# Where the gated y of a state-space mixer is kept, and who splits off its low part

## What is computed

```
for g in 8 groups, b in 2 sequences of 512 steps:
    proj   = h @ in_proj_w.T                  # gate, channels, B, C of this group
    hid,B,C = silu(causal_conv(proj, 4 taps)) # 1024 channels; B and C have 128
    y      = Y_diag + Y_off + D * hid         # chunked scan, 16 heads of 64 channels
    yg     = y * silu(gate)
    r      = rsqrt(mean(yg*yg over the group) + eps)
    out   += (yg * gnorm_w) @ out_proj_w.T * r
```

## Time and profile before

| | before |
|---|---|
| median of 3 runs | 2004.83 us (2001.99 to 2005.57) |
| the profiled execution: its time, its span | 2006.6 us, 2004.8 us |
| TensorE busy | 1951.4 us (97%) |
| VectorE busy | 1601.0 us (80%) |
| ScalarE busy | 1484.1 us (74%) |
| GpSimd busy | 1230.7 us (61%) |
| granted TensorE clock, mean | 0.996 |
| chain of waits that ended last | PE 76%, DVE 2% |
| y_lo on VectorE (L2140) | 128 instructions, 750 ns each |

### The profile page before, as it was taken

The page is one execution under the profiler, slowest core; times in us unless marked ns, Lnnn a source line. Parts: engine busy times, 40 slices in busy tenths (PEclk is TensorE's granted clock), DMA queues, the critical chain, the costliest instruction groups (busy, mean ns, idle before and its releaser), DMA issues.

```text
span 2004.8 us, 32751 instructions
## 1 busy us (share of the span) xinstructions
PE 1951.4 (97%) x10846; PEld 1567.6 (78%) x10846; DVE 1601.0 (80%) x2979; ACT 1484.1 (74%) x2986; POOL 1230.7 (61%) x854
## 2 busy tenths in 40 slices
PE   7998999999999999999999999999999999999998
PEld 5564666677888888888888888888888888888886
DVE  7777889857777878788878787878787878787888
ACT  5345866547787878787878787878787878787876
POOL 5644777644656666666656666565656665656666
PEclk9998999999999999999999999999999999999999
DMA  5615332544434343334333333333433333433424
GB/s 194 191 55 152 100 92 88 154 149 134 129 97 132 93 132 102 125 113 127 119 115 119 106 119 106 119 118 111 128 114 115 116 109 116 156 108 117 128 92 133
DMA packets 114472, 241.74 MB, mean 121 GB/s; under 512 B 23681, under 2 KB 24706, under 8 KB 113794
## 3 DMA queue, kind: packets, MB, share of 16 engines
q1 hardware_dynamic: 110466, 227.06, 36.2%
q0 software_dynamic: 3840, 12.59, 2.2%
HBM read 226.75 MB, written 12.85 MB: 120 GB/s over the span
## 4 chain that ended last, share of the span: by engine, by line
PE 76%; DVE 2%; ACT 0%; issue 0%; DVEq 0%; ACTq 0%
PE s_ps L75 13%; PE s_ps L77 13%; PE s_ps L76 13%; PE s_ps L1871 6%; PE s_ps_o L75 6%; PE s_ps_o L77 6%; PE s_ps_o L76 6%; PE s_ps L1835 5%; PE s_ps L1879 4%; PE s_ps L1827 3%; PE s_ps L1813 1%; PE s_ps L1861 0%; DVE s_cv L2110 0%; PE s_ps L1819 0%; DVE s_state L2086 0%
## 5 line engine op out<-in xcount | busy, mean ns | idle before, releaser
L2292 POOL TENSOR_TENSOR w_lo<-w_raw,w_hi 128x1024 fp32r<-128x1024 f32 x142 | 340.0, 2399 | 529.7 <-ACT w_hi L1942 529.7
L75 PE MATMUL s_ps<-h_hi,w_hi 128*128 128x512 f32 x1152 | 463.0, 402 | 6.0 <-DVE s_hid L2115 4.2
L77 PE MATMUL s_ps<-h_hi,w_lo 128*128 128x512 f32 x1152 | 450.1, 391 | 0.0
L76 PE MATMUL s_ps<-h_lo,w_hi 128*128 128x512 f32 x1152 | 448.7, 390 | 0.0
L2110 DVE SCALAR_TENSOR_TENSOR s_cv<-s_ps,s_par,s_cv 128x511 f32<-128x511 f32 (+2 forms) x480 | 355.8, 744 | 15.2 <-ACT s_cv L1985 9.3
L2309 POOL TENSOR_TENSOR s_lm<-s_lm,s_cbt 128x512 f32<-128x512 f32 x256 | 326.2, 1296 | 12.2 <-ACT s_lm L1967 12.2
L1960 ACT ACTIVATE s_lm<-s_rows,s_steps 128x128 f32<-128x128 f32 x1024 | 312.5, 391 | 0.8 <-PE s_ps L1871 0.8
L1985 ACT ACTIVATE s_cv<-s_ps,s_par 128x512 f32<-128x512 f32 x160 | 124.5, 778 | 215.8 <-PE s_ps L77 215.8
L75 PEld LDWEIGHTS s_ps<-h_hi,w_hi 128*128 128x128 f32 x1152 | 216.4, 188 | 53.9 <-DVE s_hid L2115 5.6
L77 PEld LDWEIGHTS s_ps<-h_hi,w_lo 128*128 128x128 f32 x1152 | 216.2, 188 | 47.3
L76 PEld LDWEIGHTS s_ps<-h_lo,w_hi 128*128 128x128 f32 x1152 | 216.8, 188 | 41.1
(11 more groups left out here) (295 smaller groups left out, 4106.3 us busy)
## 6 DMA issues: line engine op xcount, KB each, us to landing
w_raw<-in_w_in SPq DMA_DIRECT2D x144, 512.0 KB, 3.7
s_rows<-acs_dram SPq DMA_DIRECT2D x256, 256.0 KB, 4.6
s_wo_raw<-in_w_out SPq DMA_DIRECT2D x128, 256.0 KB, 3.5
w_raw<-in_gu_q SPq DMA_DIRECT2D x14, 512.0 KB, 3.6
f_d_q<-in_d_q SPq DMA_DIRECT2D x28, 256.0 KB, 2.7
f_d_w<-in_d_s SPq DMA_DIRECT2D x28, 256.0 KB, 3.5
table<-shifted SPq DMA_DIRECT2D x16, 256.0 KB, 2.7
xs<-in_x SPq DMA_DIRECT2D x8, 256.0 KB, 6.5
```

The source lines that it names most:

```text
L75: nc.tensor.matmul(dst, l_hi, r_hi, start=start, stop=False)
L76: nc.tensor.matmul(dst, l_hi, r_lo, start=False, stop=False)
L77: return nc.tensor.matmul(dst, l_lo, r_hi, start=False, stop=stop)
L2292: nc.gpsimd.tensor_tensor(w_lo[:, slot, :], w_raw[:, slot, :], w_hi[:, slot, :].bitcast(F32), ALU.subtract).then_inc(w_lo_ready, 1)
```

## The change

`dve_y_gated` now writes its result to SBUF, over the channel tile `hid[:, k, :]` that `dve_y_skip` has read for the last time, where before it wrote back into the DIAG bank. `y_hi` and `sq` read it there. In all units but the last, ScalarE then multiplies that tile in place by `gnorm_w` (`act_scaled`, a new instruction behind `act_sq`), and GpSimd forms `y_lo` as a plain difference (`pool_y_lo`, new); VectorE no longer does. In the last unit `y_lo` stays on VectorE and there is no `act_scaled`. The DIAG bank is free once `y_gated` is done (`y_ready`). `dve_silu` of a channel tile waits until `y_lo` of the tile that it overwrites is done.

```
-        freed = {**took, "DIAG": y_lo_ready, "H": tile_ready, "SQ": ssq_took}
+        freed = {**took, "DIAG": y_ready, "H": tile_ready, "SQ": ssq_took}
...
+        def act_scaled(act, un, k):
+            nc.scalar.activation(gated(un, k), gated(un, k), ACT.Copy,
+                                 scale=par[:, un.b, 58 + k:59 + k]).then_inc(scaled_ready, 1)
...
                     act_sq(act, un, k)
+                    if not un.last:
+                        act_scaled(act, un, k)
...
         def dve_silu(dve, v, i, th):
             dve.wait_ge(th_ready, v.at(NCONV, i))
+            if CONVS[i] >= 2 and not v.first:
+                dve.wait_ge(y_lo_ready, (v.u - 1) * KC + CONVS[i] - 1)
...
         def dve_y_lo(dve, un, k):
-            if un.last and k == KC - 1:
-                dve.wait_ge(y_hi_ready, un.at(KC, k))
-            else:
-                dve.wait_ge(sq_ready, un.at(KC, k))
+            dve.wait_ge(y_hi_ready, un.at(KC, k))
...
         def gated(un, k):
-            return tg[:] if un.last and k == KC - 1 else bank(un, ("DIAG", 0, k))
+            return hid[:, k, :]
...
-                if un.scans:
+                if un.last:
                     dve_y_lo(dve, un, k)
...
         def pool_sum(pool, un, k):
-            pool.wait_ge(sq_ready, un.at(KC, k))
+            pool.wait_ge(scaled_ready, un.at(KC, k))
...
+        def pool_y_lo(pool, un, k):
+            pool.wait_ge(scaled_ready, un.at(KC, k))
+            nc.gpsimd.tensor_tensor(y_lo[:, k % 2, :], gated(un, k), y_hi[:, k % 2, :].bitcast(F32),
+                                    ALU.subtract).then_inc(y_lo_ready, 1)
...
                     pool_wo(pool, un, k)
+                    if not un.last:
+                        pool_y_lo(pool, un, k)
                     if k and not (un.last and k == KC - 1):
                         pool_sum(pool, un, k)
```

More of the change, by code:

```diff
@@ L1589, in mixer @@
         y_lo_ready = sem("s_y_lo_ready")
-        sq_ready = sem("s_sq_ready")
+        scaled_ready = sem("s_scaled_ready")
         ssq_ready = sem("s_ssq_ready")
@@ L1932, in pe_last @@
                 if t == 0:
-                    pe.wait_ge(sq_ready, v.at(KC, KC - 1))
+                    pe.wait_ge(scaled_ready, v.at(KC, KC - 1))
                     pe_squares(sq[:, (KC - 1) % 2, :], sums, False, True).then_inc(ssq_done, 1)
@@ L2013, in act_sq @@
                 act.wait_ge(ssq_ready, un.u * (KC - 1))
-            nc.scalar.activation(sq[:, k % 2, :], gated(un, k), ACT.Square).then_inc(sq_ready, 1)
+            ins = nc.scalar.activation(sq[:, k % 2, :], gated(un, k), ACT.Square)
+            if un.last:
+                ins.then_inc(scaled_ready, 1)
+        def act_scaled(act, un, k):
+            nc.scalar.activation(gated(un, k), gated(un, k), ACT.Copy,
+                                 scale=par[:, un.b, 58 + k:59 + k]).then_inc(scaled_ready, 1)
         def act_wo(act, un, k):
@@ L2191, in gated @@
         def gated(un, k):
-            return tg[:] if un.last and k == KC - 1 else bank(un, ("DIAG", 0, k))
+            return hid[:, k, :]
         def dve_y_gated(dve, un, k):
             dve.wait_ge(y_chain, (un.u * KC + k) * 2 + 2)
-            if un.last and k == KC - 1:
-                dve.wait_ge(took["G"], UNITS * KC)
             nc.vector.tensor_tensor(gated(un, k), bank(un, ("DIAG", 0, k)), gate[:, k, :],
```

## The result

The changed kernel takes 2022.88 us, the median of four runs (2021.81 to 2025.46). The kernel before takes 2004.56 us (2001.99 to 2005.57; four runs on the same chip, three of which were those known ahead of the prediction). The ratio is 1.0095, with a 95% interval of 1.0078 to 1.0113: 18.3 us slower. The forecast was 2023 us.

What follows compares the result with a forecast made beforehand. The prediction took the mixer to be bound by TensorE, with ScalarE's full stretches in slots 0 and 2 passed on to it. Its terms sum to 17.9 us: 2024.5 for the profiled execution, 2023 us for the median, range 2011 to 2031.

Steps and rivals of the forecast that it cites:

- x: Delay per slot on ScalarE from the new activation and two reads from SBUF: 0.70 us, bounds 0.48 and 0.85.
- Slot 2: C's tap, convolutions and `silu` come later and TensorE's last projection waits: 0.71 us in each of 15 units, 10.6 us.
- Slot 1: Slot 0's gate waits for its tanh on ScalarE, delaying `yoff`, ST and T: 0.35 us in 14 units, 4.9 us.
- The -0.4 us for DIAG: DIAG no longer waits for `y_lo` to free its bank: a gain counted as 0.4 us in all.
- GpSimd: Its 120 new differences fit into its waits for `w_hi`: cost nothing, at most 0.5 x 14 = 7 us.
- The last unit: `y_lo` on VectorE, both inputs in SBUF, and GpSimd delay each other; GpSimd's round grows to 6.9: 2.5 us, bounds 0 and 8.
- The sums of unit 14: Four VectorE sums on L1723 in unit 14 meet a busier GpSimd: 0.3 us more.
- The sum: All terms over the kernel: 10.6 + 4.9 - 0.4 + 2.5 + 0.3 = 17.9 us slower.
- hidden: Rival, 7%: ScalarE's wait for TensorE covers the activation in slot 2 too; only the gate's 0.35 or less remains; 2004 to 2008.
- VectorE's release decides: Rival, 6%: the activation costs ScalarE almost nothing, freed VectorE brings slot 1's gate and `yoff` forward: 4.2 us faster, 2000.5.
- GpSimd is late: Rival, 7%: `y_lo` misses slot 1's output product or its port waits reach VectorE in all units: up to 7 us more, 2030.

Runs made afterwards that it cites:

- two-scalings kernel: The changed kernel with a second activation of the same form ahead of the in-place scaling in units 0 to 11, its output unread; ratio 1.0157 to the kernel before.
- three moves: The changed kernel with C's tap (slot 2) and the gate's tanh (slot 0) ahead of `y_hi`, and the last unit's y in PSUM; ratio 0.9978 to the kernel before.
- the early tap: The kernel before, with the tap of C ahead of `y_hi` and the square on ScalarE in slot 2; ratio 1.0067, and 0.9987 with `y_lo` behind C's `silu`.

## Why the prediction was right, step by step

**x, the delay on ScalarE**: 0.70 us predicted. By the groups (against the earlier trace rows):

```profile
L2005 ACT ACTIVATE s_y_hi<-s_hid,s_par 128x512 fp32r<-128x512 f32 x128 | 90.9, 710 | 10.5 <-DVE s_hid L2205 10.4
L2019 ACT ACTIVATE s_hid<-s_hid,s_par 128x512 f32<-128x512 f32 x120 | 85.0, 708 | 0.0
L2014 ACT ACTIVATE s_sq<-s_hid 128x512 f32<-128x512 f32 x128 | 78.8, 616 | 0.0
```

The activation takes 708 ns, 718 had been taken from the nearest row. The sources cost 40 and 29 ns (670 to 710, 587 to 616), 0.07 us where 0.08 stood. Measured from start to start it is 0.61 + 0.07 = 0.68.

**Slot 2**: 0.71 us in each of 15 units was predicted, 0.70 is the mean of 14 of them. The steps between (tap, first convolution behind the tap, `silu`, weight load) are all there, and the wait for the `silu` of C rose to 1.0 us as told. Moving the scaling behind the tap gave back 0.63, doubling it in the two-scalings kernel cost another 0.61.

**Slot 1**: 0.35 predicted, 0.33 measured. It is a difference of two effects, and both are seen apart: without the scaling the slot gains 0.28, with it alone in the kernel before it loses 0.26. A second scaling, with no gain left to set against it, cost 0.59. The -0.4 us for DIAG can't be told from the scatter. Before, its weight load waited for `y_lo` three times, 0.5 us in all, always in slot 1, and after never; that gain is inside the 0.33. Slots 1 and 2 give 14 x 0.33 + 15 x 0.70 = 15.1 us and the units grew by 14.8; of the 0.2 to 0.3 us between, 0.15 are a single slot 7, that of unit 7.

**GpSimd**: nothing predicted, nothing found; the kernel without scaling keeps all 120 differences, and its units are shorter than before. The `y_lo` of slot 0 ran at 1177.63 for 1.28 us, while the output product of slot 1 began at 1179.94, a margin of 1.03 us.

**The last unit**: 2.5 us predicted, 3.4 measured, and this is the term whose path was wrong. The prediction had GpSimd's round grow to 6.9 us and DIAG wait for GpSimd's matrices. The round grew, by 0.46 to 6.67, and two slots took its length (4 and 5; 5 and 6 had been named). But DIAG waited for nothing. TensorE waited at the output product, for `y_lo` on VectorE (4.7 us over 6 times, before 2.0 over 2), which had waited for GpSimd. By the ends in slots 2 to 5, `y_lo` ends 0.55 us behind the instruction of GpSimd that it met. The Trainium skill ("SBUF — State Buffer", section "SBUF: two separate sides") states an exclusive lock of the shared ports for a whole instruction, between GpSimd and a VectorE instruction with two SBUF inputs. The trace agrees on both sides: `y_lo` at up to 1.53 us in these slots (1.78 in slot 7) for 0.74, the next GpSimd instruction at 1.75 for 1.32; and it agrees where `y_lo` has one input in PSUM, at 0.74 us in slots 3 to 6 beside a GpSimd that runs throughout.

**The sums of unit 14** (0.3 us predicted) cost nothing. They went down (against the earlier trace rows):

```profile
L1723 DVE TENSOR_TENSOR xs<-xs,s_end_x x4: 796/798/1652, 1906.6 to 1941.2; 128x512 f32<-128x512 f32 x4
```

Their median went from 1400 to 798 ns. The first begins at 1906.6 and the last at 1941.17, and each meets the very end of GpSimd's new difference (1905.60 to 1906.89, and 1940.13 to 1941.42); it ends 0.5 us behind that. The second does the same; the third, at 1929.47, meets the instruction behind the difference near its start, and takes 1.65 us. A busier GpSimd doesn't mean longer waits; it depends on when the two meet.

**The sum**: 17.9 us predicted, 18.2 found in the traces, 18.3 in the medians. The misses of the last unit (+0.9) and of the rest (-0.6) nearly cancel, so the total is closer than the terms are, and that closeness is in part luck.

**The rivals**: "hidden" fell, since there is no idle time ahead of the tap of C. "VectorE's release decides" named a real gain, 0.28 us in slot 1, but it needed x below 0.17, and x is 0.68. "GpSimd is late" did not happen: its `y_lo` made the output product of slot 1, and its port waits reached VectorE in the last unit alone (and on L1723), where `y_lo` is VectorE's own.

## What to carry to other kernels

An engine that is busy for 80% can still have no room at one point: look for idle time directly ahead of the instruction that others wait for, not at the share. Place new work behind that instruction, into the idle time which follows; here the same activation cost 0.63 us a unit ahead of the tap and nothing behind it. And when an instruction is moved forward on one engine, follow what it pushes back onto the other engines' queues first: the early tap cost 1.0 us until `y_lo` was moved too.

## What the runs showed of the hardware

The half clock. TensorE's granted clock fell to 0.5, the lower level of 1.2 GHz, in slot 1 of the last unit in every profiled execution here, for 3.4 us, and in two kernels for 6.8 (once in two pieces). It follows on slot 0 of that unit, in which TensorE is busy for 6.4 of 8.5 us, and where it comes late in slot 1, also on a stretch there in which TensorE is busy for 3.0 of 5.7 us (three moves). It falls once more behind TensorE's last matmul, for the last 2.1 to 3.4 us of each execution (from 2002.1 us before, from 2017.0 after), which costs TensorE nothing. What the stretch in slot 1 costs depends on where in the slot it lies. The changed kernel, slots 0 and 1 of the last unit:

```profile
1953.55:1962.00 8.45, 6.36 (x49) 5.21 (x48) 6.69 (x14) 7.76 (x17) 4.38 (x4) 1.00 0.00 0
1962.00:1970.77 8.77, 7.54 (x46) 6.29 (x45) 8.01 (x17) 6.88 (x16) 5.46 (x4) 0.81 0.77 241
```

The kernel with three moves, slot 1 (its slot 0 takes 8.46 us too):

```profile
1948.53:1958.86 10.33, 7.65 (x47) 6.16 (x45) 7.98 (x17) 8.40 (x19) 5.75 (x5) 0.83 0.66 229
```

And the kernel with the scaling behind the tap:

```profile
1958.07:1969.65 11.58, 8.86 (x46) 7.08 (x45) 8.00 (x17) 9.25 (x20) 7.37 (x6) 0.71 0.70 229
```

The output product of this slot waits for `y_lo`. In the changed kernel:

```profile
1967.52 0.47 PE L75 MATMUL s_ps_o<-s_wo_hi,s_y_hi 128*128 128x512 f32 x1 [1.23 <-DVE s_y_lo L2148]
```

And with three moves:

```profile
1954.01 0.59 PE L75 MATMUL s_ps_o<-s_wo_hi,s_y_hi 128*128 128x512 f32 x1 [2.66 <-DVE s_y_lo L2154]
```

It begins 5.5 us into the slot in both. In the first the half-clock stretch begins 0.4 us into the slot. TensorE's jobs ahead of the output product take longer, its wait shrinks to 1.23 us, and the slot takes 8.8 us. In the second the stretch begins 5.7 us into the slot, in the dense matmuls of the output product, which then start 0.43 us apart in place of 0.23, and the slot takes 10.3. In the third it lasts 6.8 us and the slot takes 11.6. TensorE has the same jobs in this slot in all three, but each kernel was profiled once, so whether a kernel has a place of its own for it or it varies by execution stays open. Up to 3.5 us of a last unit may so be due to the clock (69.9 against 66.4 us with the same code); comparisons of last units here are made between executions with the stretch at the same place.
